# A transformer with eight routed experts on one core: Silu made of the hyperbolic tangent and one more step on VectorE, halved contractions, 129 columns, a new order

## The reference

```python
mod = (_silu(L0_c) @ L0_wmod).reshape(16, 6, 1, -1)
sa, ca, ga, sb, cb, gb = (mod[:, k] for k in range(6))
ga, gb = ...                                    # kept at least 0.25 away from zero
h = _layernorm(x) * (1 + ca) + sa
x = x + ga * encoder(h)                         # 4 layers, below
h = _layernorm(x) * (1 + cb) + sb
x = x + gb * ffn(h)

# one encoder layer: d = 128, 16 heads of 8, 256 tokens
h = _layernorm(x, ln1_s, ln1_b)
q, k, v = h @ Wq + bq, h @ Wk + bk, h @ Wv + bv
qp, kp = elu(q) + 1, elu(k) + 1
kv = einsum('bshd,bshm->bhmd', kp, v); ksum = sum(kp, axis=1)
att = einsum('blhd,bhmd,blh->blhm', qp, kv, 1 / (einsum('blhd,bhd->blh', qp, ksum) + 1e-6))
x = x + (att @ Wo + bo)
x = x + relu(_layernorm(x, ln2_s, ln2_b) @ W1 + b1) @ W2 + b2     # hidden width 512

# ffn: a shared expert of width 128, and 8 experts of width 64 of which each token takes its top 2
shared = (silu(x @ shared_gate) * (x @ shared_up)) @ shared_down
coef = softmax(x @ router), all but the top 2 of each token set to 0
routed = sum over e of coef[:, e] * ((silu(x @ gate[e]) * (x @ up[e])) @ down[e])
```

## Time and profile before

| | |
|---|---|
| runs of the kernel before | 589.15 us median of 3 (588.89 to 590.75) |
| the profiled execution | 587.52 us |
| its span, first to last instruction | 585.7 us |
| TensorE busy | 563.1 us (96%) |
| VectorE busy | 429.4 us (73%) |
| ScalarE busy | 395.4 us (68%) |
| GpSimd busy | 258.6 us (44%) |
| granted TensorE clock | 1.00 |

### The profile page before, as it was taken

One profiled execution on the slowest core, in us unless ns is written; L12 is line 12 of the kernel. 1 busy time (PEld: TensorE's weight loads), 2 busy tenths in 40 slices (PEclk: granted clock), 3 DMA queues, 4 the chain that ended last, 5 costly groups with the idle time before them and its releaser, 6 DMA issues.

```text
span 585.7 us, 13150 instructions
## 1 busy us (share of the span) xinstructions
PE 563.1 (96%) x4572; PEld 535.2 (91%) x4572; DVE 429.4 (73%) x1479; ACT 395.4 (68%) x1395; POOL 258.6 (44%) x431
## 2 busy tenths in 40 slices
PE   6899999999999999998999999999999999999997
PEld 3588999989999999998999999998999999999896
DVE  6967777678976777777886777767997666666785
ACT  3887688876666656787585566686686656666651
POOL 4443767464132465554412546545414334445420
PEclk9999999999999999999999999999999999999999
DMA  7700613100000000000000000000000000000000
GB/s 231 210 2 2 217 32 135 47 1 2 20 17 4 1 2 2 1 2 2 15 7 19 1 2 2 1 0 2 1 20 19 2 2 1 1 2 2 1 20 18
DMA packets 11049, 15.60 MB, mean 27 GB/s; under 512 B 960, under 2 KB 8224, under 8 KB 10600
## 3 DMA queue, kind: packets, MB, share of 16 engines
q1 hardware_dynamic: 8904, 12.54, 6.9%
q0 software_dynamic: 448, 1.25, 0.8%
q10 hardware_dynamic: 1632, 0.98, 0.6%
HBM read 12.63 MB, written 2.14 MB: 25 GB/s over the span
## 4 chain that ended last, share of the span: by engine, by line
PE 87%; ACT 6%; DVE 3%; issue 2%; POOL 1%; ACTq 1%; DVEq 0%; POOLq 0%
PE psB L1610 21%; PE psA L1610 20%; PE psD L1610 20%; PE psC L1610 18%; PE psC L1682 1%; PE psB L1682 1%; PE psD L1682 1%; PE psA L1682 1%; ACT L522 1%; ACT L476 1%; PE psD L1733 1%; PE psC L1733 1%; PE psB L1733 1%; PE psA L1733 1%; POOL xA L837 1%
## 5 line engine op out<-in xcount | busy, mean ns | idle before, releaser
L839 POOL TENSOR_TENSOR rstdD<-msD,neghalf 128x2 f32<-128x2 f32 x20 | 14.1, 704 | 54.1 <-ACT ziD L468 38.7
L839 POOL TENSOR_TENSOR rstdA<-msA,neghalf 128x2 f32<-128x2 f32 x20 | 14.1, 703 | 49.8 <-ACT eqkA L468 43.1
L1610 PE MATMUL psB<-w,H 128*128 128x128 f32 x256 | 31.7, 277 | 0.0
L1610 PE MATMUL psD<-w,H 128*128 128x128 f32 x256 | 31.3, 276 | 0.0
L1610 PE MATMUL psA<-w,H 128*128 128x128 f32 x256 | 31.2, 275 | 0.0
L1610 PE MATMUL psC<-w,H 128*128 128x128 f32 x256 | 31.2, 275 | 0.0
L1610 PEld LDWEIGHTS psC<-w,H 128*128 128x128 f32 x256 | 30.0, 192 | 0.0
L1610 PEld LDWEIGHTS psA<-w,H 128*128 128x128 f32 x256 | 30.0, 192 | 0.0
L1610 PEld LDWEIGHTS psD<-w,H 128*128 128x128 f32 x256 | 29.8, 191 | 0.0
L1610 PEld LDWEIGHTS psB<-w,H 128*128 128x128 f32 x256 | 29.8, 191 | 0.0
L839 POOL TENSOR_TENSOR rstdC<-msC,neghalf 128x2 f32<-128x2 f32 x20 | 13.9, 696 | 35.8 <-ACT eqkC L468 35.4
(11 more groups left out here) (584 smaller groups left out, 2357.6 us busy)
## 6 DMA issues: line engine op xcount, KB each, us to landing
M<-modulation_rows SPq DMA_DIRECT2D x2, 1280.0 KB, 9.5
M<-modulation_rows SPq DMA_DIRECT2D x1, 2560.0 KB, 8.6
out<-X SPq DMA_DIRECT2D x16, 128.0 KB, 1.9
M<-in_attn_W SPq DMA_DIRECT2D x3, 256.0 KB, 3.8
X<-in_attn_x_in ACTq DMA_DIRECT2D x2, 256.0 KB, 3.6
M<-in_attn_W ACTq DMA_DIRECT2D x1, 256.0 KB, 4.0
wo<-in_attn_Wo POOLq DMA_DIRECT2D x1, 256.0 KB, 4.4
wm<-in_wmod SPq DMA_DIRECT2D x1, 256.0 KB, 4.1
```

The costliest lines, as they stand in the source:

```text
L839: pool.tensor_tensor(b.rstd[:, :], b.ms[:, :], neghalf[:, :], ALU.pow).then_inc(b.s_rstd.sem, 1)
L1610: return pe.matmul(o, lhsT, rhs, start=start, stop=stop)
```

## The change

The part by part list, with what each touches:

- `silu` on ScalarE computes tanh(x/2) with the function Tanh. A new step `half_gate` on VectorE makes (tanh(x/2) + 1) times x, in place, with x read from the gate's PSUM bank. `gate_up` multiplies by 0.5 and the up, as a scalar_tensor_tensor where it was a tensor_tensor. `spread` waits for `half_gate`, not for `silu`.
- `sums` multiplies 129 columns in place of 144, one column of ones. `masked` becomes two instructions: the 128 columns times the mask, and the 16 columns of the mask times the one column of sums.
- `contract` and `down` are called in halves, each with its own wait. The first half of `contract` needs only the first half of the hidden units.
- The order of the calls is new on all four engines.

```diff
-EXPERT_UNITS = ("product2", "product0", "weighed0", "product1", "weighed1")
+EXPERT_UNITS = ("half2", "product2", "half0", "product0", "weighed0", "half1", "product1", "weighed1")
...
                 act.activation(b.eqk[:, :, :].rearrange("p a t -> p (a t)")[:, 0:width], b.ps[:, bank, 0:width],
-                               ACT.Silu).then_inc(b.s_eact.sem, 1)
+                               ACT.Tanh, scale=0.5).then_inc(b.s_eact.sem, 1)
...
             def masked(b, i, l):

                 dve.wait_ge(b.s_linps.sem, b.s_linps.value(i, 2 * l + 1))
-                dve.tensor_tensor(b.kv[:, :], b.ps[:, 1, 0:VW], headmask, ALU.mult).then_inc(b.s_kv.sem, 1)
+                dve.tensor_tensor(b.kv[:, 0:D], b.ps[:, 1, 0:D], headmask[:, 0:D], ALU.mult)
+                dve.tensor_scalar(b.kv[:, D:VW], headmask[:, D:VW], b.ps[:, 1, D:D + 1], None, ALU.mult)\
+                    .then_inc(b.s_kv.sem, 1)
...
+            def half_gate(b, i, k):
+
+                dve.wait_ge(b.s_eact.sem, b.s_eact.of(EXPERT_ACT, f"silu{k}", i))
+                width, bank = (2 * T, 1 - k) if k < PAIRS else (T, 0)
+                t = flat(b.eqk[:, :, :])[:, 0:width]
+                dve.scalar_tensor_tensor(t, t, 1.0, b.ps[:, bank, 0:width], ALU.add, ALU.mult).then_inc(b.s_units.sem, 1)
+
             def gate_up(b, i, k):

                 dve.wait_ge(b.s_eps.sem, b.s_eps.of(EXPERT_PS, f"up{k}", i))
-                dve.wait_ge(b.s_eact.sem, b.s_eact.of(EXPERT_ACT, f"silu{k}", i))
+                dve.wait_ge(b.s_units.sem, b.s_units.of(EXPERT_UNITS, f"half{k}", i))
                 if k < PAIRS:
                     if k > 0:
                         dve.wait_ge(b.s_units.sem, b.s_units.of(EXPERT_UNITS, f"weighed{k - 1}", i))
-                    dve.tensor_tensor(flat(b.gu[:, :, :]), flat(b.eqk[:, :, :]), b.ps[:, k, :], ALU.mult)\
+                    dve.scalar_tensor_tensor(flat(b.gu[:, :, :]), flat(b.eqk[:, :, :]), 0.5, b.ps[:, k, :], ALU.mult, ALU.mult)\
                         .then_inc(b.s_units.sem, 1)
...
-                    last = mm(b.ps[:, 1, 0:VW], b.kp[:, t, :], b.v[:, t, :], start=t == 0, stop=t == TILES - 1)
+                    last = mm(b.ps[:, 1, 0:D + 1], b.kp[:, t, :], b.v[:, t, 0:D + 1], start=t == 0, stop=t == TILES - 1)
...
-            def contract(b, i, l):
-                pe.wait_ge(b.s_h.sem, b.s_h.value(i, (l + 1) * PAIRS))
-                if i == 0:
+            def contract(b, i, l, k):
+
+                pe.wait_ge(b.s_h.sem, b.s_h.value(i, l * PAIRS + k + 1))
+                if i == 0 and k == 0:
                     pe.wait_ge(s_w2, 2 * l + 2)
                 for t in range(TILES):
-                    for c in range(CH):
+                    for c in (2 * k, 2 * k + 1):
...
             def spread(b, i, k):
                 pe.wait_ge(b.s_eact.sem, b.s_eact.of(EXPERT_ACT, "coefT", i))
-                pe.wait_ge(b.s_eact.sem, b.s_eact.of(EXPERT_ACT, f"silu{k}", i))
+                pe.wait_ge(b.s_units.sem, b.s_units.of(EXPERT_UNITS, f"half{k}", i))
...
-            def down(b, i):
-                order = (CH,) + tuple(range(CH))
-                pe.wait_ge(b.s_units.sem, b.s_units.of(EXPERT_UNITS, "product1", i))
-                for c in order:
-                    if c == 2:
-                        pe.wait_ge(b.s_units.sem, b.s_units.of(EXPERT_UNITS, "weighed1", i))
+            def down(b, i, part):
+
+                if part == 0:
+                    pe.wait_ge(b.s_units.sem, b.s_units.of(EXPERT_UNITS, "product1", i))
+                else:
+                    pe.wait_ge(b.s_units.sem, b.s_units.of(EXPERT_UNITS, "weighed1", i))
+                for c in ((CH, 0, 1), (2, 3))[part]:
```

Of the new order these lines of TensorE's list show the manner. First the halves among the attention's output:

```diff
                 out_project2(C, i, 0)
+                contract(B, i, 0, 0)
                 if i == 0:
                     fold_weights(4)
-                attend(D_, i, 0)
-                contract(B, i, 0)
                 out_project(D_, i, 0)
+                contract(B, i, 0, 1)
                 transposes(A, i, 2)
+                out_project2(D_, i, 0)
                 transposes(C, i, 1)
-                out_project2(D_, i, 0)
```

More of the change, by code:

```diff
@@ L669, in _ @@
                 transposed(C, i, 5)
-                squares(D_, i, 6)
                 key_exps(A, i, 3)
@@ L1505, in _ @@
                 positive_keys(C, i, 3)
+                move(B, i, 7)
                 positive_queries(C, i, 3)
@@ L1534, in _ @@
                 route(AB, i, 1)
+                half_gate(B, i, 2)
+                half_gate(A, i, 2)
                 move(D_, i, 8)
+                gate_up(B, i, 2)
                 gate_up(A, i, 2)
-                gate_up(B, i, 2)
                 weights(AB, i)
+                half_gate(B, i, 0)
+                half_gate(A, i, 0)
                 gate_up(B, i, 0)
@@ L1836, in down @@
                         hid = b.h[:, c, tok] if c < CH else b.hs[:, tok]
-                        last = mm(b.ps[:, 1, tok], hid, wd[:, c, :], start=c == order[0] and t == 0,
-                                  stop=c == order[-1] and t == TILES - 1)
-                last.then_inc(b.s_eps.sem, 1)
+                        last = mm(b.ps[:, 1, tok], hid, wd[:, c, :], start=c == CH and t == 0,
+                                  stop=c == CH - 1 and t == TILES - 1)
+                if part == 1:
+                    last.then_inc(b.s_eps.sem, 1)
             condition()
@@ L1923, in _ @@
                     fold_weights(7)
+                transposes(A, i, 3)
                 project_keys(C, i, 1)
@@ L1999, in _ @@
                 attend(A, i, 3)
-                contract(C, i, 2)
+                contract(C, i, 2, 0)
+                contract(C, i, 2, 1)
+                transposes(D_, i, 5)
+                sums(B, i, 3)
                 out_project(A, i, 3)
                 expand(D_, i, 2, 0)
-                sums(B, i, 3)
                 expand(D_, i, 2, 1)
@@ L2094, in _ @@
                     attend(B, i + 1, 0)
+                    attend(A, i + 1, 0)
+                coef_transposes(C, i)
+                up(D_, i, 1)
                 spread(C, i, 0)
-                if i + 1 < STEPS:
-                    sums(A, i + 1, 0)
                 gate(C, i, 1)
                 if i + 1 < STEPS:
-                    attend(A, i + 1, 0)
-                up(D_, i, 1)
-                if i + 1 < STEPS:
                     out_project(B, i + 1, 0)
-                up(C, i, 1)
+                spread(D_, i, 1)
+                down(D_, i, 0)
                 if i + 1 < STEPS:
```

519 lines of the change are left out of this document (272 added, 247 removed).

## The result

The changed kernel takes 598.38 us (median of 4 runs, 598.11 to 600.15), the kernel before in the same session 589.02 us (588.00 to 590.75). The ratio is 1.0162, with a 95% interval of 1.0135 to 1.0188: slower by 1.6%. The prediction was 597.4 us, in a range of 588.5 to 605, with 0.79 on slower. The profiled execution has a span of 596.3 us against 585.7.

A forecast was written before the change was run, and what follows sets the result against it. TensorE is full on average (96% busy), but VectorE nearly fills the expert stretch (32.0 of 35.4 us). 12.0 - 2.1 - 2.2 - 0.8 + 1.3 = +8.2 us on 589.15 gives 597.4 us, range 588.5 to 605.

The forecast's parts named there:

- The stretch: Experts, routing to last weighing, 35.4 us: VectorE's added 6.2 us, less mainly 2.3 us of filled waits, lengthens it 3.9 us.
- signs: Profile after: stretch 39 to 40 us, VectorE over 95% busy, TensorE idle 4 us or more, steps about 141 us.
- Around the stretch: Before and behind the expert stretch: routing comes 0.4 us later, the next step's first transposes 0.3 us sooner after the weighing.
- The junction: From the last weighing to the next step's first transposes: 2.9 us in place of 3.2, so -0.3 us.
- 129 columns: TensorE's 256 sums instructions save 0.0095 us each; -2.1 us, with the second masking instruction hidden outside the expert stretch.
- Halved contractions: Halves between out_project and out_project2 cover TensorE's 0.27 us copy wait, two places a step, eight in all: -2.2 us.
- The start: Selectors' copy on GpSimd goes behind the fold matrices, for one of which TensorE waited: -0.8 us, bounds -1.5 and +1.
- The last step: Experts from 547.9 us on: +2.6 us after filling idle time, -1.3 us as half of down(C) is left: +1.3 us.
- Table loads: 21 loads, 27 us, leave ScalarE, but it does not end the expert stretch, so they are no term of the sum.
- A (the room suffices): Rival: late work slides into the layers, the expert stretch keeps 35.4 us, the kernel gets faster, 580 us; chance 0.14.
- B's account of the stretch: Rival: all 3.4 us filled, expert stretch grows 2.5 us, -5 us elsewhere, time 589 to 591 us; chance 0.09.
- C: Rival: the second instruction of masked puts off 56 attends by 0.15 us each, 606 us; chance 0.07.

The follow-up runs named there:

- new_double: Changed kernel with one more VectorE instruction, a maximum over the same columns, in front of each half_gate; 624.60 us.
- new_two: Changed kernel with the next step's low_part calls ahead of two half_gate calls, and out_project2(A) behind out_project(B) in the start; 598.89 us.
- new_order: Changed kernel with half_gate(B, 1) ahead of weigh(A, 0), and A's next-step bias, move, squares and root ahead of B's; 598.72 us.
- new_short: Changed kernel with half_gate on 16 columns in place of 512 or 256, its instructions, waits and order kept; 594.37 us.
- new_whole: Changed kernel with every contraction whole again, the down products still halved; 604.34 us.
- old_tanh: Kernel before with Tanh and half_gate alone, each call put where its operand is needed; 631.28 us.
- old_cols: Kernel before with only the 129 columns and the masking in two instructions; 589.78 us, ratio 1.0016.
- old_swap: Kernel before with GpSimd's selector behind the fold matrices and the last layer's transposes(C) ahead of out_project2(D); 588.64 us, ratio 0.9994.
- new_silu: Changed kernel with Silu back on ScalarE and half_gate gone, new order, 129 columns and halved calls kept; 634.16 us.

## Why the prediction was right, and where not

*The stretch* (+3.9 us predicted, +2.7 measured) is the main term, and its mechanism holds at its upper side: VectorE is 97% busy, more work costs its full time (new_double), and moving single waits changes nothing (new_two, new_order). The size of the work was off: VectorE's busy time grew by 4.9 us, not by 6.2. Its rows in the stretch add up to 39.4 us before and 46.7 after, and 7.1 of these 7.4 us are `half_gate`; but they also overlap by 2.5 us more. The new instructions' own overlaps, 0.08 us each, are 1.0 of it. The rest comes from instructions that stood apart before and now stand back to back, so the room was larger than the idle time. That idle time was right: 3.4 less 1.2 makes 2.2 us filled, and 2.3 had been taken. But the prediction spoke as if this work were all; new_short shows that 1.8 of the 2.7 us stay when 4.0 us of it go. The prediction names TensorE's new waits ("its `spread` and, through `gate_up`, its `up` now wait for this step too") and gives them no term. How much of the 1.8 is theirs and how much the order's stays open. Of the signs that it named, VectorE over 95% busy, layers 1 us shorter and `half_gate` rows of 0.68 and 0.42 us came; but the stretch is 38.1 us and not 39 to 40, TensorE idles 2.4 us of it and not 4, and a step takes 139.9 us and not 141.

*Around the stretch* (+0.4 and -0.3): the first was no cost. Half of D's contraction ahead of `logits2(B)` is part of what the halves gain, as new_whole shows. The junction is shorter by 0.1 us, not 0.3; with A's calls ahead of B's (new_order) A's transposes come another 0.65 us earlier behind the last weighing, so B's squares and root were in their way.

*129 columns* (-2.1 us): the columns are faster, but the step that failed is the cost of the second masking instruction, "one more small instruction for each call of `masked` hides there". It does not where GpSimd adds a bias, nor at two places of a step where TensorE comes right behind it. The saving itself was taken low, 0.0095 us for each instruction where 0.011 were measured. In the order before nothing is gained, in the new one 0.5 to 1 us.

*Halved contractions* (-2.2 us): the sum was too small. By the distances between starts the kernel before loses 0.30 us at each such place, not 0.27, and in the changed kernel four of the seven places in a step no longer lose it: the two that were counted, by the halves (new_whole brings them back), and two more, which stay covered in new_whole and so owe it to the order of the other calls. Of the 6.0 us that new_whole lost, 1.5 are the two counted places in the three steps, 3.0 are in the four stretches, around the gates, where I had seen only a delay, and 1.5 are in the start, of which 0.5 are the same two places.

*The start* (-0.8 us, +1.15 measured with the first layers): the wait for the fold matrix went, and waits of `out_project2` came in its place. How much of the 1.15 is the change's stays open. old_tanh issues the same instructions as the kernel before up to the first routing, and reaches it at 136.12, 1.5 us later than the profiled execution of before; one row of each shows one reason (19 to 24 us, the clock is the number behind the counts):

```profile
19.00:24.00 5.00, 4.07 (x26) 3.27 (x27) 4.67 (x14) 4.78 (x19) 2.04 (x4) 1.00 0.90 272
```

```profile
19.00:24.00 5.00, 4.37 (x23) 4.18 (x21) 3.56 (x11) 3.84 (x14) 3.24 (x6) 0.66 0.91 274
```

The start differs between executions by more than this term. old_cols (135.73) and old_swap (135.93), whose starts are nearly that of before, are late too, so the profiled execution of before had an early one; old_cols shows no lower clock there, so the clock is not all of it.

*The last step* (+1.3 us, +2.9 measured): the stretch there grew by 3.4 us, not 2.6, and the half of `down(C)` gave back 0.5 us, not 1.3.

*Table loads*: 21 loads leave, and are no part of the sum, as predicted. What the prediction did not see is that the new order rests on their absence: with Silu, and without the further step, its span is 36 us longer (632.2 against 596.3).

The rivals: A (the room suffices) is refuted by the result and by old_tanh; B's account of the stretch (+2.5 us) is nearest to the measured 2.7, but the 5 us that it took off elsewhere are not there; C names the right place at the wrong breadth: 5 of the small instructions collide in the changed kernel, 8 in old_cols, and not 56. The total is as near as it is by luck (+8.2 us predicted, +9.4 measured between the medians, +10.6 between the spans) for errors met: each of three steps was taken 0.8 us too long, and the start and the last step together 4.6 us too short. Of the range's own ends, the lower one (593) takes both bounds together; the upper one by the same sum is 606, not 605.

## What to carry to other kernels

Price added work on an engine that is nearly full from both sides: here the next microsecond costs about one, and the one taken away gives back 0.2, because waits stand just below. Judge an engine whose rows overlap by the distances between starts as well: TensorE's rows hid most of 0.30 us at each of six places in a step, and VectorE's overlapped by 2.5 us more once there was more to do. And don't expect a gain from mending a single wait while the engine behind it is full. A function that spares table loads is worth what the order can do with it; judged in the old order, it loses.

## What the runs showed of the hardware

- A VectorE TENSOR_SCALAR of 128x16, with its tensor in SBUF and its scalar in PSUM, lasted until the end of the GpSimd addition of 128x256 in which it started in 8 of 8 cases (old_cols): 0.52 to 0.66 us in place of 0.23. In the changed kernel one that started 0.07 us before such an end lasted through the next addition, 0.76 us.
- A wait of TensorE's weight load cost time that the matmuls' rows hardly show: the next matmul started 0.31 us after the last in place of 0.11, and the one behind it after 0.21 (the kernel before, 186.27 us), while the rows leave 0.04 us uncovered.
- TensorE's granted clock fell to 0.50 (1.2 GHz) after it had been busy 0.43 of 2 us, and stayed there for some 7 us (new_double); in the start it was 0.66 over 5 us in one execution and 1.00 in another of the same instructions.
- ScalarE loaded its table eight times in 14 us (308.9 to 322.8 us of new_silu), 1.28 us each, and the activation behind each load started 1.29 us after the load did.
